# A two-layer attention kernel: 64-column score tiles, exponentials in halves, and one vector operation for maximum and bias

## The reference, cut to what matters

```python
def layer1(x, Wq, bq, Wk, bk, Wv, bv, gamma):
    q = (x @ Wq + bq).reshape(b, n, c)
    k = (x @ Wk + bk).reshape(b, n, c)
    v = (x @ Wv + bv).reshape(b, n, c)
    energy = einsum('bic,bjc->bij', q, k)
    attn = softmax(energy, axis=-1)
    out = einsum('bmn,bmc->bnc', attn, v)
    return gamma * out.reshape(b, h, w, c) + x
```

## Time and profile before

| | |
|---|---|
| median of 3 runs | 4641.6 us (4641.44 to 4648.05) |
| the profiled execution, own time | 4663.67 us |
| its span | 4661.8 us |
| busy share PE / DVE / ACT / POOL | 95% / 76% / 61% / 39% |
| mean granted TensorE clock | 0.936 of full |

### The profile page before, as it was taken

The page is one execution under the profiler, slowest core; times in us unless marked ns, Lnnn a source line. Parts: engine busy times, 40 slices in busy tenths (PEclk is TensorE's granted clock), DMA queues, the critical chain, the costliest instruction groups (busy, mean ns, idle before and its releaser), DMA issues.

```text
span 4661.8 us, 74927 instructions
## 1 busy us (share of the span) xinstructions
PE 4416.2 (95%) x21608; PEld 1379.6 (30%) x21608; DVE 3521.5 (76%) x6665; ACT 2843.7 (61%) x3762; POOL 1826.5 (39%) x845
## 2 busy tenths in 40 slices
PE   5998999989999999999999999999999989999899
PEld 3224222242222422233222422224222242222422
DVE  4776887768777687767877688775887768877687
ACT  1575666746566566655667566674666756666565
POOL 1692008910099001970039600494006930079200
PEclk7898999979999799998999899997999979999799
DMA  0000000000000000000000000000000000000000
GB/s 28 1 10 19 0 0 10 10 19 0 10 1 10 19 0 9 1 19 10 0 10 1 21 7 0 10 1 28 0 0 10 10 19 0 0 10 10 19 0 9
DMA packets 13505, 40.00 MB, mean 9 GB/s; under 512 B 2621, under 2 KB 2621, under 8 KB 10813
## 3 DMA queue, kind: packets, MB, share of 16 engines
q1 hardware_dynamic: 13244, 36.78, 2.6%
HBM read 19.99 MB, written 8.39 MB: 6 GB/s over the span
## 4 chain that ended last, share of the span: by engine, by line
PE 50%; DVE 25%; issue 18%; ACT 3%; DVEq 1%; POOL 1%; SPq 0%; ACTq 0%; POOLq 0%; DMA 0%
PE sum_banks L431 17%; DVE chunk_max L932 17%; PE score_banks L411 9%; PE score_banks L508 5%; PE score_banks L509 4%; PE sum_banks L520 3%; PE sum_banks L453 3%; PE score_banks L584 2%; PE score_banks L360 2%; DVE exp_bias L935 2%; PE sum_banks L383 2%; ACT e_whole L704 1%; PE score_banks L345 1%; DVE tile_max L773 1%; POOL e_sum L312 1%
## 5 line engine op out<-in xcount | busy, mean ns | idle before, releaser
L312 POOL TENSOR_TENSOR e_sum<-e_sum,e_whole 128x1024 f32<-128x1024 f32 x704 | 1659.4, 2357 | 91.7 <-ACT e_whole L645 40.7
L704 ACT ACTIVATE e_whole<-score_banks,exp_bias,down 128x1024 f32<-128x1024 f32 x1024 | 1232.5, 1204 | 751.6 <-DVE exp_bias L935 751.3
L773 DVE TENSOR_REDUCE tile_max<-sum_banks 128x1 f32<-128x512 f32 (+1 forms) x2128 | 1365.2, 686 | 429.5 <-PE sum_banks L383 426.2
L645 ACT ACTIVATE e_whole<-score_banks,no_bias,down 128x1024 f32<-128x1024 f32 x1024 | 1228.9, 1204 | 552.5 <-PE score_banks L411 540.5
L932 DVE TENSOR_REDUCE chunk_max<-score_banks 128x1 f32<-128x1024 f32 x1024 | 1251.4, 1222 | 221.9 <-PE score_banks L509 208.4
L431 PE MATMUL sum_banks<-e_whole,proj 128*64 128x512 f32 x4096 | 1123.2, 628 | 0.0
L520 PE MATMUL sum_banks<-e_whole,v_scaled 128*64 128x512 f32 x4096 | 1095.8, 617 | 6.6 <-DVE v_scaled L922 6.6
L309 POOL TENSOR_TENSOR e_sum<-e_whole 128x1024 f32<-128x1024 f32 x32 | 75.4, 2356 | 2085.9 <-ACT e_whole L645 2085.9
L508 PE MATMUL score_banks<-k_high,q_split 128*128 128x512 f16 x2048 | 798.6, 390 | 63.2 <-ACT e_whole L704 23.4
L509 PE MATMUL score_banks<-k_low,q_split 128*128 128x512 f16 x2048 | 788.1, 385 | 0.0
L383 PE MATMUL sum_banks<-f_tr,g_tr 33*128 33x512 f16 x2128 | 699.7, 402 | 22.1 <-DVE tile_max L773 18.3
(11 more groups left out here) (112 smaller groups left out, 2080.3 us busy)
## 6 DMA issues: line engine op xcount, KB each, us to landing
x_in<-in_x_dram SPq DMA_DIRECT2D x19, 1024.0 KB, 4.8
out_dram<-x_mid SPq DMA_DIRECT2D x32, 256.0 KB, 2.2
k_high<-k_high SPq DMA_DIRECT2D x32, 128.0 KB, 2.2
k_low<-k_low SPq DMA_DIRECT2D x32, 128.0 KB, 2.2
gammas<-in_L_conv_gamma_dram SPq DMA_DIRECT2D x2, 0.5 KB
w<-in_L_conv_wg_dram SPq DMA_DIRECT2D x1, 2.0 KB
w<-in_L_conv_bg_dram SPq DMA_DIRECT2D x1, 0.0 KB
w<-in_L_conv_wf_dram SPq DMA_DIRECT2D x1, 2.0 KB
```

The source lines that it names most:

```text
L312: nc.gpsimd.tensor_tensor(acc, acc, e_whole[:, i % U0, :], ALU.add).then_inc(e_added, 1)
L645: nc.scalar.activation(e_whole[:, i % U0, :].rearrange("p (a n) -> p a n", a=2), score_banks[:, 2 * (i % 2):2 * (i % 2) + 2, :], ACT.Exp, ...
L704: nc.scalar.activation(e_whole[:, u, :].rearrange("p (a n) -> p a n", a=2), score_banks[:, 2 * (u % 2):2 * (u % 2) + 2, :], ACT.Exp, bias= ...
L773: nc.vector.reduce_max(tile_max[:, blk, j:j + 1], sum_banks[:, (2 + j % banks) % 4, :], AX_X).then_inc(a_used, 1)
```

## The change

In layer 1 alone:

- `scores1` makes each 128-column matmul into two with 64 columns of `q_split` as stationary operand, which write partitions 0 to 63 and 64 to 127 of the same bank. So eight matmuls per step, in the order high, high, low, low for each bank. It waits for each bank apart.
- ACT's exponential becomes two of 512 columns, one per bank, each with its own row sum and its own count on `exp1_done` (which now counts to 2 per step; the starting credit goes from 2 to 4).
- DVE's maximum and the offset behind it become one `tensor_scalar`, which multiplies the scores by `neg_down`, takes the minimum along the way into `exp_bias`, and writes the 1024 products into `o_tr`, where nobody reads them.
- Per tile, `row_max1` and `below_max` become one minimum over four offsets; ACT takes the subtraction into its exponential's scale and bias. The row sum goes over 8 partial sums.
- PE's loop over `t` is written out 16 times.

```diff
-    FREE_ST, FREE_A, FREE_E0, FREE_S1, FREE_E1 = 2, 4, U0, 2, U1
+    FREE_ST, FREE_A, FREE_E0, FREE_S1, FREE_E1 = 2, 4, U0, 4, U1
...
+        scaled = o_tr[:, :, :].rearrange("p (b a) n -> p b (a n)", b=2)
...
             def scores1(image, i, k, u):
-                pe.wait_ge(exp1_done, image * STEPS1 + k + 1)
                 for h in range(2):
+                    pe.wait_ge(exp1_done, 2 * (image * STEPS1 + k) + h + 1)
                     col = (u % NCH) * CH + h * BANK
                     bank = score_banks[:, 2 * (u % 2) + h, :]
-                    nc.tensor.matmul(bank, q_split[:, ds(i * P, P)], k_high[:, col:col + BANK], start=True, stop=False)
-                    mm = nc.tensor.matmul(bank, q_split[:, ds(i * P, P)], k_low[:, col:col + BANK],
-                                          start=False, stop=True)
+                    for k_part in (k_high, k_low):
+                        for c in range(2):
+                            mm = nc.tensor.matmul(bank[c * C:(c + 1) * C, :], q_split[:, i * P + c * C:i * P + (c + 1) * C],
+                                                  k_part[:, col:col + BANK], start=k_part is k_high, stop=k_part is k_low,
+                                                  skip_group_check=True)
                 mm.then_inc(s_ready, 1)
...
-                pe.wait_ge(exp1_done, image * STEPS1 + t * U1 + u + 1 + FREE_S1)
+                pe.wait_ge(exp1_done, 2 * (image * STEPS1 + t * U1 + u + 1) + FREE_S1)
...
-                steps1(0, True)
-                with pe.Fori(1, T // 2) as t:
-                    steps1(t, False)
+                for t in range(T // 2):
+                    steps1(t, t == 0)
...
-                        nc.scalar.activation(e_whole[:, u, :].rearrange("p (a n) -> p a n", a=2),
-                                             score_banks[:, 2 * (u % 2):2 * (u % 2) + 2, :],
-                                             ACT.Exp, bias=exp_bias[:, u:u + 1], scale=down[:, 0:1],
-                                             accum_out=part_sum[:, u // NCH, u % NCH:u % NCH + 1]
-                                             ).then_inc(exp1_done, 1)
+                        for h in range(2):
+                            nc.scalar.activation(e_whole[:, u, h * BANK:(h + 1) * BANK], score_banks[:, 2 * (u % 2) + h, :],
+                                                 ACT.Exp, bias=exp_bias[:, u:u + 1], scale=down[:, 0:1],
+                                                 accum_out=part_sum[:, u // NCH, u % NCH, h:h + 1]
+                                                 ).then_inc(exp1_done, 1)
...
-                            nc.scalar.activation(chunk_w[:, odd, :], below_max[:, odd, :], ACT.Exp
-                                                 ).then_inc(chunk_w_ready, 1)
+                            nc.scalar.activation(chunk_w[:, odd, :], exp_bias[:, odd * NCH:(odd + 1) * NCH], ACT.Exp,
+                                                 scale=-1.0, bias=neg_row1[:, odd:odd + 1]).then_inc(chunk_w_ready, 1)
...
-                        chain.link(nc.vector.reduce_max(chunk_max[:, odd, j:j + 1],
-                                                        score_banks[:, 2 * (u % 2):2 * (u % 2) + 2, :]
-                                                        .rearrange("p a n -> p (a n)"), AX_X))
-                        nc.vector.tensor_scalar(exp_bias[:, u:u + 1], chunk_max[:, odd, j:j + 1], neg_down[:, 0:1],
-                                                None, ALU.mult).then_inc(bias_ready, 1)
+                        nc.vector.tensor_scalar(scaled[:, u % 2, :], score_banks[:, 2 * (u % 2):2 * (u % 2) + 2, :]
+                                                .rearrange("p a n -> p (a n)"), neg_down[:, 0:1], None, ALU.mult, ALU.min,
+                                                accum_out=exp_bias[:, u:u + 1]).then_inc(bias_ready, 1)
                         if j == NCH - 1:
-                            chain.link(nc.vector.reduce_max(row_max1[:, odd:odd + 1], chunk_max[:, odd, :], AX_X))
-                            nc.vector.tensor_scalar(below_max[:, odd, :], chunk_max[:, odd, :],
-                                                    row_max1[:, odd:odd + 1], down[:, 0:1], ALU.subtract, ALU.mult
-                                                    ).then_inc(below_ready, 1)
+                            dve.wait_ge(bias_ready, k + 1)
+                            nc.vector.tensor_reduce(neg_row1[:, odd:odd + 1], exp_bias[:, odd * NCH:(odd + 1) * NCH],
+                                                    AX_X, ALU.min).then_inc(row_ready, 1)
```

More of the change, by code:

```diff
@@ L146, in attention_pair_kernel @@
         neg_down = sb("neg_down", [P, 1], F32)
-        chunk_max = sb("chunk_max", [P, 2, NCH], F32)
         exp_bias = sb("exp_bias", [P, U1], F32)
-        row_max1 = sb("row_max1", [P, 2], F32)
-        below_max = sb("below_max", [P, 2, NCH], F32)
+        neg_row1 = sb("neg_row1", [P, 2], F32)
         chunk_w = sb("chunk_w", [P, 2, NCH], F32)
-        part_sum = sb("part_sum", [P, 2, NCH], F32)
-        part_scr = sb("part_scr", [P, NCH], F32)
+        part_sum = sb("part_sum", [P, 2, NCH, 2], F32)
+        part_scr = sb("part_scr", [P, NCH, 2], F32)
         row_sum1 = sb("row_sum1", [P, 2], F32)
@@ L176, in attention_pair_kernel @@
         s_ready, bias_ready, exp1_done, pv1_done = sem("s_ready"), sem("bias_ready"), sem("exp1_done"), sem("pv1_done")
-        below_ready, chunk_w_ready, y_ready = sem("below_ready"), sem("chunk_w_ready"), sem("y_ready")
+        row_ready, chunk_w_ready, y_ready = sem("row_ready"), sem("chunk_w_ready"), sem("y_ready")
         dve_step = sem("dve_step")
@@ L473, in chunk0 @@
                 if q == 0:
-                    pe.wait_ge(exp1_done, image * STEPS1 + FREE_S1)
+                    pe.wait_ge(exp1_done, 2 * image * STEPS1 + FREE_S1)
                 pe.wait_ge(mrow_sb, image * NCH + q + 1)
@@ L757, in _ @@
             LINK_PIECES, LINK_MAX, LINK_ATT = 6, 2, 1
-            LINK_BOUND, LINK_CHUNK, LINK_BELOW, LINK_W = 8, 1, 1, 3
-            LINK_BLOCK = NCH * LINK_CHUNK + LINK_BELOW + LINK_W
+            LINK_BOUND, LINK_W = 8, 3
+            LINK_BLOCK = LINK_W
             L0 = NCH * (LINK_MAX + LINK_ATT)
@@ L909, in weigh_chunks @@
                     dve.wait_ge(chunk_w_ready, image * T + i + 1)
-                    dve.wait_ge(exp1_done, image * STEPS1 + (i + 1) * NCH + FREE_S1)
+                    dve.wait_ge(exp1_done, 2 * (image * STEPS1 + (i + 1) * NCH) + FREE_S1)
                     chain.link(nc.vector.tensor_tensor_reduce(
-                        out=part_scr[:, :], in0=part_sum[:, par, :], in1=chunk_w[:, par, :], scale=1.0, scalar=0.0,
+                        out=part_scr[:, :, :], in0=part_sum[:, par, :, :],
+                        in1=chunk_w[:, par, :].unsqueeze(2).to_broadcast([P, NCH, 2]), scale=1.0, scalar=0.0,
                         op0=ALU.mult, op1=ALU.add, accum_out=row_sum1[:, par:par + 1]))
@@ L918, in weigh_values @@
                 def weigh_values(i, par):
+                    chain.wait()
                     dve.wait_ge(pv1_done, image * NCH * T + i * NCH + FREE_E1 - NCH)
@@ L959, in image_steps @@
                 weigh_chunks(T - 1, 1)
-                chain.wait()
                 weigh_values(T - 1, 1)
```

2 lines of the change are left out of this document (1 added, 1 removed).

## The result

The changed kernel takes 4519.2 us (median of 4 runs, 4512.38 to 4529.35) against 4641.5 us of the kernel before in the same session: ratio 0.9737, 95% interval [0.9724, 0.9751]. That is 122 us less; forecast were 133 less and 4509 us, range 4427 to 4591.

What follows compares the result with a forecast made beforehand. Layer 1 was held bound by PE's list and the score-bank loop, both 1.98 us a step. Step 2.03 to 1.90 (loop 1.87 plus 0.03 DVE), 0.13 x 1024 = 133 us: 4641.6 - 133 = 4509 us, range 4427 to 4591.

Steps and rivals of the forecast that it cites:

- Two bounds at once: Layer 1: PE's own instruction list and the loop over the score banks each take 1.98 us a step; shortening one brings next to nothing.
- late maxima: DVE's maximum starting late behind the tile's weights, 0.15 once in four steps; forecast 0.07 late, 0.03 us a step.
- The tiles: Layer 1 matmuls all in 64-column tiles: two shape-change losses go, 0.19 a step; PE's instructions then take 1.75 to 1.80.
- rival 3: Layer 1 scores: float16 halves do not run side by side; 614 us slower, about 5256; chance 0.06.
- rival 2: PE's weight loads show, 0.05 for each score pair; 1.96 a step, 4570 us; chance 0.10.
- The fused operation: DVE's maximum and offset as one operation: 1.28 us, between 1.22 and 1.43, saving 0.19 in two steps.
- Rival 4: DVE's fusion takes the old two operations' time or more: at 1.43, 4591 us; at 1.54 no gain; chance 0.07.
- rival 1: Score-bank loop shorter still: no pointer price (1.22), load hidden, no extras; 3.64 for two steps, 4427 us; chance 0.10.
- The bank loop: Layer 1, from scores through DVE and ACT back to PE's scores two steps later: 3.75 for two steps, 1.87 a step.
- the 4-element chunk weight on ACT: Layer 1, ACT's small operation once in four steps: claimed to lie in room, with no time added.
- What the halves lose on ACT they win on PE: Two half exponentials free the second bank 0.37 later, but PE's scores behind the wait shrink by 0.38.
- The sign in the waits: Profile after the change: PE's score loads should wait for the exponential of the second bank, not the first.

## Why the prediction was right

- **Two bounds at once: shown.** Tiles alone gave 11 us, the fusion alone stopped at PE's 1.979, both together 152 us (4642 to 4490). "Next to nothing" for one alone held for the tiles and the halves, not for the fusion. The fusion gave 71 us. What was mis-sized there is the late maxima: the expectation left part of them on top of PE's list, but what shortens the loop also gives DVE room, and so all of them went: 2.036 - 1.979 = 0.057 a step, 58 us. The prediction had also read one late start of 0.15 from the earlier trace rows; the trace of before has four in a pass of 8 steps, of 0.12 to 0.36.
- **The tiles: shown.** 0.19 was forecast for the two changes of shape and 1.75 to 1.80 for PE's list; measured 0.257 and 1.722. The uncovered weight load ahead of the values (0.05) belongs to the price of the change of shape and was not counted there. Pairs of float16 run side by side: rival 3 is out. So is rival 2: the 64-column weight loads, without the fast load that the Trainium skill's "TensorEngine Tiling (Array Packing)" says column tiling turns off ("Restrictions and Gotchas"), take 0.11 where 128 columns took 0.10, which fits, and hide under the running pair.
- **The fused operation: 1.282 against 1.28.** Rival 4 is out, and so is rival 1's price without the pointer (1.22). The version without it shows that it is the part on which the rest hangs.
- **The bank loop was mis-sized: 3.75 forecast, 3.67 measured.** Halves start 0.77 apart (0.79 taken), the second's read ends 0.86 after its start (0.88), PE starts 0.05 behind (0.07) and needs 0.24 to its last pair (0.27). The loop lies nearer rival 1's 3.64 than the forecast's sum.
- **The late maxima were mis-sized the other way: 0.03 a step forecast, 1.904 - 1.837 = 0.067 measured.** The forecast had the tile's work follow DVE's operation at once, in 0.66, and 0.59 free. The term that failed is "the 4-element chunk weight on ACT", put among what lies in room: DVE waits for it 0.40, since ACT reaches it later behind two halves, then works 0.55, and from the end of the operation to the next one are 561.30 - 560.34 = 0.96. The two errors, -0.04 and +0.04 a step, cancel: 1.90 forecast, 1.904 measured. The hit on the step is in part luck.
- **"What the halves lose on ACT they win on PE"** was right for the loop (they even win 0.10 in two steps) and wrong for the kernel: they cost 30 us through DVE's wait for the chunk weight.
- **The sign in the waits** came out for the matmuls and not for the count. The loads wait at both banks (157 times), but of the 0.16 a step that PE stands still, 0.14 are at the second bank: the second bank's wait decides, as the prediction had it. A count of the loads' waits can't show this, nor could the 66 waits of the earlier trace rows: in the earlier trace rows the scores at 507.10 stand just where PE's own list has them.

In the traces layer 1 is 129 us shorter, against 133 forecast: the 15 passes behind the first give 0.132 a step, the first pass of each image only 0.36 us instead of 1.06. The other 7 us to the 122 measured are less than the spread of the runs (4512 to 4529).

## What to carry to other kernels

Write down the engine's own list and the buffer loop side by side before costing an edit: where both are equal, a part that shortens one pays little beyond the late starts that it removes (11, 15 and 71 us here), and only the pair pays in full (152). Then look at the engine in the loop that also has occasional work: whether that work fits between two of its turns, and when its input comes, can cost more than the loop wins, and moving it to an idle engine gave 60 us here where moving it in a kernel without late starts gave nothing. When a change has three parts, run it without each; here one of the three was a loss until another engine was freed, and the version without the tiles was not run. Where a profile counts waits of weight loads, look whether the matmuls stand still as well.

## What the runs showed of the hardware

- A change between 128-column and 64-column tiles costs PE 0.257 us there and back at the upper clock level, weight load included; a change between float16 and float32 in the same shape costs nothing (0.215 from the last score pair to the values).
- Two float16 matmuls with 64 columns each and 128 rows, 512 columns moving, start 3 to 8 ns apart and take 0.215 together, as one with 128 columns does (0.216).
- DVE's multiply with a running minimum over 1024 columns of PSUM, with the products written to SBUF, takes 1282 ns against 1222 of the plain maximum, and 0.01 more until the minimum is there.
- The chunk weight's exponential with a scale of -1 and a per-partition offset takes 0.29 where it took 0.19 with neither.
- GpSimd's operations on 1 to 8 columns take about 0.20, on 256 columns 0.61, and DVE's operation next to them kept its length: 1284 ns in the 240 operations that overlap the scaled values on GpSimd, and 1284 in the rest.
